# A four-layer graph network kernel: degrees turned through DRAM as 32 partitions of 16 values instead of 128 of 4

## What is computed

```python
def _sage_conv(x, src, dst, Wl, Wr, b):
    agg = segment_sum(x[src], dst, num_segments=n)
    deg = segment_sum(ones_like(dst), dst, num_segments=n)
    mean = agg / maximum(deg, 1.0)[:, None]
    return mean @ Wl + x @ Wr + b
h = maximum(layernorm(x), 0.0)
h = relu(_sage_conv(h, src, dst, Wl1, Wr1, b1))   # 256 -> 256
h = relu(_sage_conv(h, src, dst, Wl2, Wr2, b2))   # 256 -> 128
h = relu(_sage_conv(h, src, dst, Wl3, Wr3, b3))   # 128 -> 256
return x + _sage_conv(h, src, dst, Wl4, Wr4, b4)  # 256 -> 256
```

## Time and profile before

| | |
|---|---|
| median of 3 runs | 666.85 us (663.74 to 667.23) |
| span of the profiled execution | 659.6 us; no time of its own is listed beside it |
| median less that span | 7.25 us |
| PE busy | 622.7 us (94%) |
| DVE busy | 276.2 us (42%) |
| ACT busy | 179.1 us (27%) |
| POOL busy | 42.8 us (6%) |
| the chain that ended last | PE 78%, DMA 7%, DVE 7%, ACT 3% |
| of it `rdeg_d<-newH` (L850) | 3% |
| of it `rdeg_d<-rdeg` (L845) | 2% |

### The profile page before, as it was taken

One profiled execution on the slowest core, in us unless ns is written; L12 is line 12 of the kernel. 1 busy time (PEld: TensorE's weight loads), 2 busy tenths in 40 slices (PEclk: granted clock), 3 DMA queues, 4 the chain that ended last, 5 costly groups with the idle time before them and its releaser, 6 DMA issues.

```text
span 659.6 us, 10093 instructions
## 1 busy us (share of the span) xinstructions
PE 622.7 (94%) x4071; PEld 345.0 (52%) x4072; DVE 276.2 (42%) x526; ACT 179.1 (27%) x381; POOL 42.8 (6%) x91
## 2 busy tenths in 40 slices
PE   5679998899999899998999999899999999999998
PEld 4436555555554455553444444444445555646686
DVE  6978877678788779711212121111120100101011
ACT  3886854265643623210111011121110000000000
POOL 8002300000000000000000000000001011010110
PEclk9977999999999999999999999999999999999999
DMA  8301200510231122242534431445430223032030
GB/s 265 95 0 49 79 1 2 183 51 6 69 33 52 34 52 65 50 136 48 160 87 117 122 85 45 101 111 144 120 121 1 54 70 112 0 112 83 30 113 33
DMA packets 63526, 50.98 MB, mean 77 GB/s; under 512 B 35510, under 2 KB 48347, under 8 KB 63480
## 3 DMA queue, kind: packets, MB, share of 16 engines
q1 hardware_dynamic: 63124, 49.74, 26.6%
q0 software_dynamic: 240, 0.37, 0.2%
q10 hardware_dynamic: 116, 0.24, 0.1%
HBM read 28.15 MB, written 16.60 MB: 68 GB/s over the span
## 4 chain that ended last, share of the span: by engine, by line
PE 78%; DMA 7%; DVE 7%; ACT 3%; issue 2%; SPq 1%; POOL 1%; DVEq 0%; ACTq 0%; POOLq 0%
PE agg_ps L2241 27%; PE window_ps L2241 18%; PE lin_ps L2159 6%; PE lin_ps L2176 5%; PE window_ps L2072 4%; PE lin_ps L2135 3%; DMA rdeg_d<-newH 3%; PE lin_ps L2029 2%; PE window_ps L2217 2%; PE agg_ps L2217 2%; DMA rdeg_d<-rdeg 2%; DVE early L1445 1%; PE lin_ps L2263 1%; ACT counts L1794 1%; PE lin_ps L2184 1%
## 5 line engine op out<-in xcount | busy, mean ns | idle before, releaser
L2241 PE MATMUL agg_ps<-counts,H 128*128 128x512 f16 (+3 forms) x1026 | 235.0, 355 | 1.6 <-DVE aggT L1536 1.5
L2241 PEld LDWEIGHTS agg_ps<-counts,H 128*128 128x128 f16 (+1 forms) x1026 | 79.2, 98 | 56.6 <-issue 10.8
L1794 ACT ACTIVATE counts<-window_ps 128x400 f16<-128x400 f32 x150 | 73.6, 507 | 64.5 <-PE window_ps L2072 50.6
L1438 DVE TENSOR_TENSOR counts<-early 128x2048 f16<-128x2048 bf16 x66 | 77.9, 1215 | 6.3 <-PE window_ps L2072 4.8
L2241 PE MATMUL window_ps<-counts,early 128*128 128x512 f16 (+2 forms) x346 | 77.6, 379 | 0.0
L2241 PEld LDWEIGHTS window_ps<-counts,early 128*128 128x128 f16 (+1 forms) x346 | 33.7, 98 | 41.5 <-issue 3.4
L2241 PE MATMUL window_ps<-counts,H 128*128 128x512 f16 (+2 forms) x291 | 55.3, 346 | 0.0
L1536 DVE SCALAR_TENSOR_TENSOR aggT<-agg_ps,columns,rdeg 128x512 f32<-128x512 f32 (+1 forms) x27 | 16.9, 659 | 81.2 <-PE agg_ps L2241 62.6
L2072 PEld LDWEIGHTS window_ps<-counts 128*128 128x128 f16 x412 | 30.8, 99 | 34.3 <-issue 4.6
L1438 DVE TENSOR_TENSOR early<-early 128x1024 f16<-128x1024 bf16 (+1 forms) x69 | 43.8, 684 | 7.4 <-PE window_ps L2072 5.9
L2241 PE MATMUL agg_ps<-counts,early 128*128 (+4 forms) x297 | 46.5, 314 | 0.0
(11 more groups left out here) (241 smaller groups left out, 631.9 us busy)
## 6 DMA issues: line engine op xcount, KB each, us to landing
selfT<-hT_d SPq DMA_DIRECT2D x18, 512.0 KB, 4.2
hT_d<-newT SPq DMA_DIRECT2D x12, 512.0 KB, 4.5
rdeg<-rdeg_d SPq DMA_DIRECT2D x22, 256.0 KB, 4.1
counts<-in_x_dram SPq DMA_DIRECT2D x6, 512.0 KB, 7.9
hT_d<-counts SPq DMA_DIRECT2D x6, 512.0 KB, 3.4
newH<-in_x_dram SPq DMA_DIRECT2D x6, 512.0 KB
out_dram<-newT SPq DMA_DIRECT2D x5, 512.0 KB
hT_d<-newT SPq DMA_DIRECT2D x6, 256.0 KB, 3.9
```

What stands on the lines that cost most here:

```text
L1438: v.tensor_tensor(hots_of(group).rearrange("p r a (n d) -> p r a n d", d=2), pairs.unsqueeze(1).unsqueeze(1).broadcast_to([P, n, 2, P // 2 ...
L1794: a.activation(counts[:, :, 2 * w * WIN:2 * (w + 1) * WIN].rearrange("p t (a w) -> p a t w", a=2), window_bank(FILL_AT[w])[:, 0:2 * KEYS]. ...
L2241: last = m((agg_ps, window_ps)[bank][:, h, 0:n], tile[:, part, h * P:(h + 1) * P], counts[0:rows_, k, chunk_cols(c, n)], start=first and p ...
```

## The change

For q = 3 to 6 the turned degrees come back as a block of 32 partitions with 16 neighbouring values each (`ROW_PARTS` = 512 / 16 = 32), not as 128 partitions of 4 values that stand 128 apart in DRAM. The block lies in the columns that the four places' `rdeg_columns` had, 16 columns wide, and all four places share it. The load, the inversion and the store back use it. The row store, the broadcast, all waits and the order of the instructions stay as they are. The degrees of places 0 to 2 and their stores (L835) are not touched.

```diff
+        ROW_PARTS = CH // ((NCH - 3) * TPC)
+        degree_block = uppers[0:ROW_PARTS, 2 * NCH * TPC + 3 * TPC:3 * NCH * TPC]
...
-        assert len(FILLS[-1]) == 32
+        assert len(FILLS[-1]) == 32 and BY_STEPS == 3
...
-                    columns_ = rdeg_d[0, ORDER[q] * CH:(ORDER[q] + 1) * CH].rearrange("(t p) -> p t", p=P)
+                    block_ = rdeg_d[0, ORDER[q] * CH:(ORDER[q] + 1) * CH].rearrange("(p t) -> p t", p=ROW_PARTS)
                     sp.wait_ge(degrees_taken, q - BY_STEPS + 1)
                     sp.dma_start(row_, rdeg[0:1, :]).then_inc(degree_row_stored, 16)
                     sp.wait_ge(degree_row_stored, done)
-                    sp.dma_start(rdeg_columns[:, q, :], columns_, allow_slow_non_contiguous=True
-                                 ).then_inc(degree_columns_loaded, 16)
+                    sp.dma_start(degree_block, block_).then_inc(degree_columns_loaded, 16)
                     sp.wait_ge(degree_inverted, q + 1)
-                    sp.dma_start(columns_, rdeg_columns[:, q, :], allow_slow_non_contiguous=True
-                                 ).then_inc(rdeg_columns_stored, 16)
+                    sp.dma_start(block_, degree_block).then_inc(rdeg_columns_stored, 16)
                     sp.wait_ge(rdeg_columns_stored, done)
                     sp.dma_start(rdeg[:, :], row_.broadcast_to([P, CH])).then_inc(rdeg_back, 16)
...
-                v.reciprocal(rdeg_columns[:, q, :], rdeg_columns[:, q, :]).then_inc(degree_inverted, 1)
+                v.reciprocal(degree_block, degree_block).then_inc(degree_inverted, 1)
```

## The result

| | before | changed |
|---|---|---|
| median of 20 runs | 663.88 us (658.81 to 667.23) | 659.97 us (656.09 to 661.79) |
| span of the profiled execution | 659.6 us | 654.5 us |
| time of the profiled execution | not listed | 656.29 us |

The medians lie 3.9 us apart. The ratio is 0.9932, with a 95% interval of 0.9911 to 0.9954: between 3.0 and 5.9 us faster. The gain was right in size and the base was not: the three runs shown had their median 3.0 us above that of twenty.

A forecast was written before the change was run, and what follows sets the result against it. The prediction took PE, busy 622.7 of 659.6 us, as the bound. Its terms, 2.4 + 0.6 + 1.0 - 0.03 = 4.0 us, off the median 666.85 gave 662.9 us, range 661.0 to 666.1.

The forecast's parts named there:

- the base: Median of the three runs shown, 666.85 us, from which the gain was subtracted; the profiled span stood 7.25 us under it.
- The waits that the change can reach: Four PE waits in layer 1, 2.97, 0.70, 0.73 and 1.47 us, said to be all the change can reach: 5.87 us.
- The store back: Inverted values to DRAM in 32 pieces of 64 B instead of 512 of 4 B: 2.9 us instead of 9.66.
- The last place: Place 6, end of layer 1: broadcast lands earlier, PE's sums become last, PE's 2.97 us wait shrinks; gain 2.4 us.
- Place 3 to 4: Transposes no longer held by the broadcast, so DVE scales earlier and PE's wait before place 4's sums shrinks; gain 0.6 us.
- The column load: 32 pieces read instead of 512, each load 0.5 us shorter; PE's two waits before hots shrink in places 3 and 4; gain 1.0 us.
- The inversion: 32 x 16 instead of 128 x 4: about 0.02 us longer, four times, two before PE; cost 0.03 us in sum.
- The sum: Gains of 2.4, 0.6 and 1.0 less 0.03 us: 4.0 us, taken off the median to give 662.9 us.
- Rival 4: More than forecast: load loses all its 0.8 us, place 5 and hots waits give too; 5 to 6.5 us, about 661; chance 0.06.
- 1: Rival: each 64 B write costs as much as its 16 old ones; only the load's gain remains, 665.9 us; chance 0.10.
- 3: Rival: slower, as neighbouring writes hinder each other and the store grows; about 686 us; chance 0.04.
- 2: Rival: other waits replace those removed, from a full ring or slower broadcast and transposes; 1.5 to 3.2 us left; chance 0.25.

The follow-up runs named there:

- e8: Changed kernel's load and inversion (32 x 16), but the old 128 x 4 strided store back, of a constant 0.125; PE's last layer 1 wait 2.05 us.
- e9: The change in place 6 alone, places 3 to 5 as in the kernel before; ratio 0.997 (0.9933 to 1.0007) against the kernel before.
- e12: Changed kernel again, no edit, beside the kernel before on the same chip, with granted clocks recorded; 661.08 us, ratio 0.9958 (0.9931 to 0.9985).
- e4: Kernel before, but its 512 inverted values stored 64 B apart in a DRAM tensor of their own, 0.001 broadcast instead; store landed in 1.8 us.
- e6: Kernel before, but its 512 inverted values stored 8 B apart in a DRAM tensor of their own, 0.001 broadcast instead; store landed in 3.1 us.
- e2: Changed kernel's 32 partitions of 16 values, but the values 32 apart in DRAM, so 512 pieces of 4 B; store landed in 6.4 us.
- e1: Kernel before with 128 partitions of 4 neighbouring values, 128 pieces of 16 B; store landed in 1.4 us, span 660.5 us at a lower clock.
- e3: Changed kernel with 16 partitions of 32 neighbouring values, 128 B each, in a small tile of their own; store landed in 1.3 us.
- e10: The change in places 3 to 5 alone, place 6 as in the kernel before; ratio 0.9945 (0.9912 to 0.9979) against the kernel before.
- e13: Kernel before, unchanged, profiled again; span 660.2 us at mean clock 0.987, PE's last layer 1 wait 3.02 us.
- e15: Kernel before, unchanged, another profiled execution; span 665.5 us at mean clock 0.979, PE's last layer 1 wait 2.59 us.
- e14: Kernel before, unchanged, another profiled execution; span 659.6 us at mean clock 0.987, PE's last layer 1 wait 2.20 us.
- e11: Changed kernel with row store and column load issued ahead of the 512 KB feature store in places 3 to 5; 659.56 us, ratio 0.9922.

## Why the prediction was right or wrong

**The waits that the change can reach** (5.87 us of PE): right for three of them. All four fell in the changed kernel's trace, but the 0.70 us before place 4's sums is absent in e8 and e9 too (see below). Of the other waits of PE behind the turns the only one to fall by more than 0.3 us is that at 420 us, which e12 does not confirm.

**The store back**, 2.9 us forecast: 1.3 measured. The reason was wrong. The prediction priced the old store at 14 ns a write, "because the price seems to go by writes"; e4 shows 512 writes landing in 1.8 us. It is where they are written, side by side in the row just used; closeness is part of it for certain (e4 to e6). The row store, taken as the near bound, was no bound either: 1.3 us is half of it. The term held because any store below about 5.8 us was said to do; e2 bears that out with 6.4 us. That a wrong price did no harm is luck. The Trainium skill (DMA: Bandwidth & Descriptors, Specifications) has a read and a write back for anything below 512 B, and the prediction asked whether that would leave the store at 9.66 us. It does not: 16 B, 64 B and 128 B pieces land in 1.4, 1.3 and 1.3 us (e1, the change, e3). Whether the old store's closeness costs through such rewriting no run here shows.

**The last place**, 2.4 us: 2.36 in the two traces, and DVE's wait now ends with PE's sums, as said. The other traces of the kernel before have 3.02, 2.20 and 2.59, so that the average of the four is 2.70 and the term 0.3 us less; e8 and e10, with the old store there, have 2.05 and 1.46. The term was right for its trace.

**Place 3 to 4**, 0.6 us: 0.70 gone in the trace, but that the change did it is not shown. The wait was 0.71, 0.48 and 0.38 us in e13 to e15 and absent in e8 and e9, where the store back of place 3 is the old one and DVE still waits 1.11 and 1.38 us for the transposes. The path was there, the size hung on a few tenths of a microsecond. In place 4 nothing was forecast and the first trace shows nothing; e13 to e15 show PE waits of 0.4 to 1.2 us near 238 us that end with the hots behind L1510, where DVE waits 2.10 to 2.87 us (1.61 in the first trace); the changed kernel has neither. A small gain was missed there.

**The column load**, 1.0 us for two waits: 0.73 + 0.94 = 1.7 in the traces, mis-sized. The load lost 0.3 us in its median, but up to 1.0 in front of DVE (3.68 to 2.71). In e12 the first of the waits was 0.16 us, so 1.5 is fairer. The fixed cost of about 2 us that the prediction quotes is no floor here: loads landed in 1.4 us at the least and stores in 1.3.

**The inversion**, 0.02 us more: 0.06 (0.18 to 0.24). It stayed without effect.

**The sum** of 4.0 us stands well in the interval of 3.0 to 5.9. In e12's runs the change is worth 2.8 us (1.0 to 4.6). That it comes so close to the 3.9 between the medians is partly luck: the waits it is made of sum to 4.7 us in the traces, the gain at like clock is 2.6 to 3.3 in timed runs, and the scatter is as large as the difference.

**The step that failed is the base**: "Off the median: 666.85 - 4.0" and "with 0.2 us for the runs' scatter". The three runs shown spread over 3.5 us, their median was 3.0 us above the median of twenty, and the prediction read the 7.25 us between median and span as if it were fixed. It is 1.8 us (656.29 and 654.5; 662.01 and 660.2 in e13; 1.75 to 1.91 in every execution with both on record): the profiled execution was itself one of some 661.4 us. The other 5.4 us were slower executions; that they had more time at 1.2 GHz is likely, since those of 666 us and more beside e12 have a mean clock of 0.976 to 0.979, but the three have no clock on record. Against 663.88 the same sum gives 659.9, the measured time (659.97).

**The range** was built of mechanisms alone and left the scatter out, although the rows of times showed it. Rival 4's own 6.5 us would have put its edge at 660.4, not 661.0. **The rivals**: 1 and 3 fell with the store's 1.3 us. 2 is partly true in e12's smaller gain, not as a mechanism: no new wait took the old ones' place. 4 is what the two profiled traces alone would say (5.1 us), and the load did lose more than 1.0 us of PE's waits; the interval of 3.0 to 5.9 does not exclude it.

Open: why timed executions of the kernel before at 0.987 took 658.5 to 660.2 us and its three profiled ones 661.4 to 662.0 (the first from its span plus 1.8), when the changed kernel shows no such gap (656.29 profiled, 656.1 to 657.0 timed). The timed ones and e13 and e14 ran on different chips (12 and 0), and nothing here parts the chips from the profiling. In like clock the gain is therefore 2.6 us in timed runs and 5.1 in traces.

## What to carry to other kernels

When a small store of single values back to DRAM takes long although its packets are through at once, give each partition a neighbouring run (16 B were enough here) or set the values apart (64 B were enough here, in a tensor of their own). Price a removed wait on the engine that sets the end (4.7 us of PE here), never on the queue (32 us of SP), and ask what releases that engine next. And before a time is forecast to half a per cent, compare the profiled execution's own time and clock with the runs: three runs of a kernel with a spread of 0.5% are no base for it.

## What was not expected of the hardware

- 512 writes of 4 B landed in 1.8 us when 64 B apart in a tensor of their own, and in 8 to 11 us when side by side in the row just used; 128 writes of 16 B side by side in that row in 1.4 us.
- A short store from 32 partitions lands in 1.3 us. The row store of the same 2 KB from one partition takes 2.46 us with a 512 KB store right ahead of it on the queue, and 3.1 us in e11 with a 512 KB load there instead.
- Executions of one program differ by up to 9 us (658.51 to 667.64), and most of that goes with how many stretches at 1.2 GHz fall into them. One such stretch, in early layer 1, cost 2.9 us; another came right after a wait of PE of 2.59 us and cost 1.6 us on the next eight products. The changed kernel, whose wait there is 0.61 us, was in the lowest clock group in 0 of 32 executions, the kernel before in 15 of 34. But e9, with the same short wait, was there in 3 of 10, e10 in 5 of 10, and in e10 the traced drop lay at 422 us, behind another wait; three traces of the kernel before had the long wait and no drop. That the shorter wait keeps the clock up may be a part of the gain, by estimate about 1 us (15 of 34 executions times the 2.1 us between the lowest two groups of the table), and is not shown.
